# Context values and output projections of a decoder layer as three one-pass products

## The reference

```python
out = jnp.einsum('bhqk,bkhd->bqhd', attn, V).reshape(B, S, D)
return out @ Wo.T + bo                       # the output projection
...
attn = jax.nn.softmax(scores, axis=-1)       # scores of the layernormed x against the context
readout = jnp.einsum('bsm,bmd->bsd', attn, memory_tokens)   # the context values
...
x = x + attention(layernorm(x)); x = x + context(layernorm(x)); x = x + experts(layernorm(x))
```

## Time and profile before

| | us |
|---|---|
| median of 3 runs | 220.63 (220.3 to 221.02) |
| the profiled execution | 220.86, span 219.1 |
| PE busy | 211.4 (96%) |
| DVE busy | 160.7 (73%) |
| ACT busy | 129.6 (59%) |
| POOL busy | 87.5 (40%) |

### The profile page before, as it was taken

The page is one execution under the profiler, slowest core; times in us unless marked ns, Lnnn a source line. Parts: engine busy times, 40 slices in busy tenths (PEclk is TensorE's granted clock), DMA queues, the critical chain, the costliest instruction groups (busy, mean ns, idle before and its releaser), DMA issues.

```text
span 219.1 us, 4397 instructions
## 1 busy us (share of the span) xinstructions
PE 211.4 (96%) x1390; PEld 176.4 (80%) x1390; DVE 160.7 (73%) x440; ACT 129.6 (59%) x249; POOL 87.5 (40%) x77
## 2 busy tenths in 40 slices
PE   7999999999999899999999999999999999999995
PEld 2687766776787689799898898898898898898893
DVE  3469898869558657888998785785785786786754
ACT  2138789859641814468767765665676666666340
POOL 7249989304001110076347625615516516416000
DMA  6795530000000000004331342142141241310002
GB/s 208 297 377 170 145 100 0 0 3 1 3 0 0 0 3 1 0 2 148 144 84 66 140 144 81 63 144 63 80 144 41 102 144 24 120 48 0 0 0 97
DMA packets 8062, 17.45 MB, mean 80 GB/s; under 512 B 960, under 2 KB 3184, under 8 KB 7920
## 3 DMA queue, kind: packets, MB, share of 16 engines
q1 hardware_dynamic: 7616, 16.97, 23.0%
q10 hardware_dynamic: 432, 0.31, 0.5%
HBM read 16.75 MB, written 0.52 MB: 79 GB/s over the span
## 4 chain that ended last, share of the span: by engine, by line
PE 83%; DVE 8%; ACT 4%; issue 3%; POOL 1%; DVEq 0%; ACTq 0%; POOLq 0%
PE PS L1185 35%; PE PS L1201 20%; PE PS L957 3%; PE PS L1069 3%; PE PS L1054 3%; PE PS L945 3%; PE PS L1009 3%; ACT pr L458 2%; PE PS L1042 2%; PE PS L971 2%; PE PS L995 2%; PE PS L1230 2%; PE PS L1022 2%; PE PS L999 1%; DVE masked L741 1%
## 5 line engine op out<-in xcount | busy, mean ns | idle before, releaser
L320 POOL TENSOR_TENSOR WLg<-raw_g,WHg 128x1024 fp32r<-128x1024 f32 x16 | 38.4, 2399 | 69.3 <-ACT WHg L428 65.7
L1185 PE MATMUL PS<-XH,WHg 128*128 128x512 f32 x120 | 47.1, 392 | 0.0
L1185 PE MATMUL PS<-XL,WHg 128*128 128x512 f32 x120 | 46.9, 391 | 0.0
L1185 PE MATMUL PS<-XH,WLg 128*128 128x512 f32 x120 | 46.7, 389 | 0.0
L867 DVE TENSOR_SCALAR pt<-pt 128x512 f32<-128x512 f32 x30 | 23.8, 792 | 20.7 <-ACT pt L552 20.7
L1201 PE MATMUL PS<-WLd,HH 128*128 128x256 f32 x120 | 34.0, 283 | 0.0
L1201 PE MATMUL PS<-WHd,HL 128*128 128x256 f32 x120 | 33.9, 283 | 0.0
L1201 PE MATMUL PS<-WHd,HH 128*128 128x256 f32 x120 | 33.9, 282 | 0.0
L558 ACT ACTIVATE HH<-pt 128x512 fp32r<-128x512 f32 x30 | 18.9, 630 | 18.8 <-DVE pt L871 18.2
L552 ACT ACTIVATE pt<-PS,bup 128x512 f32<-128x512 f32 x30 | 20.6, 687 | 13.3 <-PE PS L1185 13.2
L871 DVE SCALAR_TENSOR_TENSOR pt<-pt 128x512 f32<-128x512 f32 x30 | 24.9, 830 | 4.2 <-DVE pt L867 1.4
(11 more groups left out here) (172 smaller groups left out, 358.5 us busy)
## 6 DMA issues: line engine op xcount, KB each, us to landing
raw_g<-we_d SPq DMA_DIRECT2D x16, 512.0 KB, 4.1
raw_w<-we_d SPq DMA_DIRECT2D x16, 256.0 KB, 2.7
ctxT<-ctxT_d SPq DMA_DIRECT2D x1, 1024.0 KB, 9.4
ctx_sb<-ctx_d SPq DMA_DIRECT2D x1, 1024.0 KB, 11.7
wqkv<-wqkv_d SPq DMA_DIRECT2D x3, 256.0 KB, 3.9
out_d<-x SPq DMA_DIRECT2D x4, 128.0 KB, 1.7
rows<-rows_d SPq DMA_DIRECT2D x1, 264.0 KB, 6.1
x<-x_d ACTq DMA_DIRECT2D x2, 128.0 KB, 2.8
```

Source lines behind the costliest of these rows:

```text
L320: g.tensor_tensor(WLg[slot][:, :, :, :].rearrange("p k g f -> p (k g f)"), raw_g[slot][:, :], WHg[slot][:, :, :, :].rearrange("p k g f -> ...
L1185: i = t.matmul(PS[:, 2 * m + part, :], w[slot][:, k, part, m * P:(m + 1) * P], xx[:, k, :], start=(n == 0), stop=(n == 3 * KD - 1))
```

## The change

- The output projection of both batches and the context values of all four chunks become three one-pass products each: high x high, low x high, high x low (for the context values: high x high and high x low of a chunk first, and its low x high later in a function of its own).
- ScalarE's copies out of PSUM are the same in number and size but now write the high part (att_high, xpt_high).
- VectorE gets seven new subtractions from PSUM for the low parts: one of 128x512 for the attention of batch 0 (`low_att`), two of 128x256 for that of batch 1, and one of 128x512 for each of the four context chunks (`context_low`).
- GpSimd rounds and subtracts wo (128x512) after the router, and the context in two halves of 128x1024 after the second key split and after rstds(1).
- TensorE no longer spreads the context values of chunks 0 and 1 in halves around project(1) and the transposes: it does the high passes of a chunk before and its low pass behind.
- The memory of the raw context and of xT is used again for the low context and for wo's parts. The transfers are not touched.

```diff
+        xpt_high, xpt_low = (sb(n, [P, 2, KM, P], F32R) for n in ("xpt_high", "xpt_low"))
...
@@ GpSimd
             split_router()
+            pool.wait_ge(wo_in, 16)
+            pool.wait_ge(v_ps, NC)
+            g.tensor_copy(wo_high[:, :, :], wo[:, :, :]).then_inc(wo_high_done, 1)
+            pool.wait_ge(wo_high_done, 1)
+            g.tensor_tensor(wo_low[:, :, :], wo[:, :, :], wo_high[:, :, :].bitcast(F32), ALU.subtract).then_inc(wo_low_done, 1)
             split_keys(0)
             masks()
             split_keys(1)
+            def split_context(b):
+
+                pool.wait_ge(ctx_in, 16)
+                chunks = slice(b * KM, (b + 1) * KM)
+                g.tensor_copy(ctx_high[:, chunks, :], ctx_sb[:, chunks, :]).then_inc(ctx_high_done, 1)
+                pool.wait_ge(ctx_high_done, b + 1)
+                g.tensor_tensor(ctx_low[:, chunks, :], ctx_sb[:, chunks, :], ctx_high[:, chunks, :].bitcast(F32), ALU.subtract
+                                ).then_inc(ctx_low_done, 1)
+
+            split_context(0)
             rstds(1)
+            split_context(1)
...
@@ VectorE
+            def low_att(b, n, bank, tokens):
+
+                if b == 1:
+                    dve.wait_ge(proj_done, QC)
+                dve.wait_ge(attT_done[b], n)
+                count = tokens.stop - tokens.start
+                v_.tensor_tensor(att_low[:, :, tokens.start - b * S:tokens.stop - b * S], PS[:, bank, 0:KD * count].rearrange("p (k n) -> p k n", k=KD),
+                                 att_high[:, :, tokens].bitcast(F32), ALU.subtract).then_inc(att_low_done[b], 1)
+
...
+            def context_low(c):
+
+                dve.wait_ge(xpt_done, c + 1)
+                if c >= 2:
+                    dve.wait_ge(xav_done, c - 1)
+                v_.tensor_tensor(xpt_low[:, c % 2].rearrange("p h q -> p (h q)"), PS[:, XT_BANK[c], :],
+                                 xpt_high[:, c % 2].rearrange("p h q -> p (h q)").bitcast(F32), ALU.subtract).then_inc(xlow_done, 1)
...
                 if v == TAIL - 1:
                     outputs(0, 0, 7)
+                if v == TAIL:
+                    low_att(0, 1, 7, slice(0, S))
...
+            context_low(0)
             context_weight(0)
             context_weight(1)
+            context_low(1)
+            low_att(1, 1, 7, slice(S, S + P))
+            low_att(1, 2, 0, slice(S + P, T))
             residual(1, 0, PS[:, 6, 0:D])
...
             normalise(x3, 3, (0, 1))
+            context_low(2)
             context_weight(2)
             context_weight(3)
+            context_low(3)
...
@@ TensorE
-                    pe.wait_ge(attT_done[b], 1 if b == 0 else j + 1)
+                    pe.wait_ge(att_low_done[b], 1 if b == 0 else j + 1)
+                    n = 0
                     for k in range(KD):
-                        i = t.matmul(places[j], attT[:, k, c * P:(c + 1) * P], wo[:, k, :],
-                                     start=(k == 0), stop=(k == KD - 1))
+                        for xx, w in ((att_high, wo_high), (att_low, wo_high), (att_high, wo_low)):
+                            chunk = j if xx is att_low else c
+                            i = t.matmul(places[j], xx[:, k, chunk * P:(chunk + 1) * P], w[:, k, :], start=(n == 0), stop=(n == 3 * KD - 1))
+                            n += 1
...
-            def context_values(c, blocks=range(KM)):
+            def context_values(c):
                 pe.wait_ge(xpt_done, c + 1)
-                for j in blocks:
...
+                pe.wait_ge(ctx_low_done, c // QC + 1)
+                for j in range(KM):
+                    for w in (ctx_high, ctx_low):
+                        t.matmul(PS[:, XV_BANK[c], 0:D], xpt_high[:, c % 2, j, :], w[:, (c // QC) * KM + j, :],
+                                 start=(j == 0 and w is ctx_high), stop=False)
+
+            def context_values_low(c):
+                pe.wait_ge(xlow_done, c + 1)
+                for j in range(KM):
+                    i = t.matmul(PS[:, XV_BANK[c], 0:D], xpt_low[:, c % 2, j, :], ctx_high[:, (c // QC) * KM + j, :],
+                                 start=False, stop=(j == KM - 1))
+                i.then_inc(xav_done, 1)
...
-            pe.wait_ge(ctx_in, 16)
-            context_values(0, range(0, KM // 2))
+            context_values(0)
             project(1, [PS[:, 6, 0:D], PS[:, 5, 0:D]])
-            context_values(0, range(KM // 2, KM))
-            context_values(1, range(0, KM // 2))
+            context_values_low(0)
+            context_values(1)
             for j in range(QC):
                 pe.wait_ge(xn_done, NC + QC + j + 1)
                 turn_chunk(xn, QC + j, (7, 3)[j])
-            context_values(1, range(KM // 2, KM))
+            context_values_low(1)
...
             context_values(2)
+            context_values_low(2)
             context_values(3)
+            context_values_low(3)
```

More of the change, by code:

```diff
@@ L65, in decoder_layer @@
         rest_of_wqkv = sb("rest_of_wqkv", [P, KD, D])
-        ctx_sb = sb("ctx_sb", [P, B * KM, D])
+        raw_ctx = ExitStack()
+        ctx_sb = raw_ctx.enter_context(nc.sbuf_tensor("ctx_sb", [P, B * KM, D], F32))
+        raw_ctx.close()
+        ctx_low = sb("ctx_low", [P, B * KM, D], F32R)
+        ctx_high = sb("ctx_high", [P, B * KM, D], F32R)
+        xpt_high, xpt_low = (sb(n, [P, 2, KM, P], F32R) for n in ("xpt_high", "xpt_low"))
         wo = sb("wo", [P, KD, D])
@@ L95, in decoder_layer @@
         xn = sb("xn", [P, NC, D])
-        xT = sb("xT", [P, KD, T])
+        turned_x = ExitStack()
+        xT = turned_x.enter_context(nc.sbuf_tensor("xT", [P, KD, T], F32))
+        turned_x.close()
+        wo_high, wo_low = (sb(n, [P, KD, D], F32R) for n in ("wo_high", "wo_low"))
         kT = sb("kT", [P, KD, T])
@@ L107, in decoder_layer @@
         att = sb("att", [P, NC, D])
-        attT = sb("attT", [P, KD, T])
+        att_high = sb("att_high", [P, KD, T], F32R)
+        att_low = sb("att_low", [P, KD, S], F32R)
         x2 = sb("x2", [P, NC, D])
@@ L163, in decoder_layer @@
         xp = [keys_flat[:, i * M:(i + 1) * M] for i in range(2)]
-        xpt = [keys_flat[:, (2 + i) * M:(3 + i) * M].rearrange("p (c q) -> p c q", q=P) for i in range(2)]
         cth, ctl = [keys_high0[:, :, :], keys_high1[:, :, :]], [keys_low[:, b * KD:(b + 1) * KD, :] for b in range(B)]
@@ L183, in decoder_layer @@
         attT_done = [sem(f"attT_done{b}") for b in range(B)]
+        att_low_done = [sem(f"att_low_done{b}") for b in range(B)]
+        wo_high_done, wo_low_done = sem("wo_high_done"), sem("wo_low_done")
         q_ps, k_ps, v_ps = sem("q_ps"), sem("k_ps"), sem("v_ps")
@@ L205, in decoder_layer @@
         out_done = sem("out_done")
+        xlow_done, ctx_high_done, ctx_low_done = sem("xlow_done"), sem("ctx_high_done"), sem("ctx_low_done")
         dbias_zero, dbias_split, score3_zero, score_parts = (sem(n) for n in ("dbias_zero", "dbias_split", "score3_zero", "score_parts"))
@@ L471, in context_take @@
                     act.wait_ge(xav_done, c - 1)
-                a.activation(xpt[c % 2].rearrange("p h q -> p (h q)"), PS[:, XT_BANK[c], :], ACT.Copy
+                a.activation(xpt_high[:, c % 2].rearrange("p h q -> p (h q)"), PS[:, XT_BANK[c], :], ACT.Copy
                              ).then_inc(xpt_done, 1)
@@ L515, in _ @@
                     act.wait_ge(lnT_done, 3)
-                    a.activation(attT[:, :, 0:S], turned(7, slice(0, S)), ACT.Copy).then_inc(attT_done[0], 1)
+                    a.activation(att_high[:, :, 0:S], turned(7, slice(0, S)), ACT.Copy).then_inc(attT_done[0], 1)
                 if v == NV:
@@ L525, in take_chunk @@
                              ).then_inc(done, 1)
-            take_chunk(attT, 2, 7, 5, attT_done[1])
-            take_chunk(attT, 3, 0, 6, attT_done[1])
+            take_chunk(att_high, 2, 7, 5, attT_done[1])
+            take_chunk(att_high, 3, 0, 6, attT_done[1])
             context_take(1)
@@ L1098, in _ @@
                 if v == TAIL + 1:
-                    pe.wait_ge(wo_in, 16)
+                    pe.wait_ge(wo_low_done, 1)
                     project(0, [PS[:, 7, j * D:(j + 1) * D] for j in range(QC)])
```

## The result

The changed kernel takes 222.11 us in the median of 6 runs (221.84 to 222.24) against 220.49 of the kernel before in the same comparison: ratio 1.007, 95% interval 1.006 to 1.008, so 1.6 us slower. The profiled execution has a span of 220.5 against 219.1.

A forecast was written before the change was run, and what follows sets the result against it. TensorE was taken to bound the kernel (83% of the chain), with VectorE nearly as late in the touched stages. Terms 0.33 + 1.20 - 0.30 = +1.23 on 220.86 gave 222.1, stated as 222.0; 8-in-10 range 221.1 to 222.8 us.

The forecast's parts named there:

- Cost of a product: TensorE's replaced products: three one-pass instructions take 0.359 us, 0.20 first and 0.1195 each later, against 0.419 for one float32 product.
- the whole possible gain: TensorE over both projections and four context chunks: 1.4 us less work, called all the change could gain.
- Batch 0, +0.33: Batch 0's projection: waits for VectorE's new subtraction, starts at 45.39 instead of 44.77, ends 0.33 us later.
- Batch 1, +1.20: Batch 1's projection: low attention queues behind chunk 1's low part on VectorE; residual 1.20 us later, arriving whole at context scores.
- Chunks 2 and 3, -0.30: Context values of chunks 2 and 3: TensorE ends 0.40 us earlier, but VectorE is late, so only 0.30 is gained.
- GpSimd at no cost: GpSimd's splits of wo and context: at most 3.3 and 4.7 us, fitting into 12 us of waiting, so free.
- The sum: Whole kernel: 0.33 + 1.20 - 0.30 = +1.23 us, from 220.86 profiled to 222.1, given as 222.0.
- The hidden low parts: Rival at batch 1's projection: low attention delivered before 63.44, TensorE's saving shows, 219.5 us; chance 0.08.
- The absorbed shift: Rival between batch 1's projection and chunk 2's context scores: only half of 1.20 arrives, 221.5 or 221.2 us; chance 0.17.
- rival 3: GpSimd's new work holds VectorE's small instructions: 0.1 us for the rstd scaling, up to 0.6 more, 222.7; chance 0.13.
- The rule of a quarter: Replaced TensorE products: three passes for float32's four would save a quarter, 2.5 us, where the rows gave one seventh, 1.4.
- What should show: Profile signs: TensorE idle 0.6 before project(0), 1.2 before project(1); residual at 65.9; wrong if chunk 2's scores under 1 us later.

The follow-up runs named there:

- e7: Changed kernel with VectorE's weights of chunks 2 and 3 moved ahead of context_low(2): 221.78 us, ratio 1.0048 to the kernel before.
- e1: Changed kernel with context_low(1) moved behind batch 1's two low attention parts on VectorE: 220.92 us against 220.67 before, ratio 1.0013.
- e2: Changed kernel with VectorE's list of batch 1 put in order of readiness: 220.66 us against 220.65 before, ratio 0.9996.
- e4: Changed kernel with only the output projections in three products, context values float32 in halves as before: 220.97 us, ratio 1.0015 to the kernel before.
- e5: Changed kernel with GpSimd's second context split moved ahead of rstds(1): 221.94 us, ratio 1.0061 to the kernel before.
- e8: Changed kernel with transposes before project(0), batch 1's list by readiness, chunk 2 and 3 weights first, early second split: 219.61 us against 220.65 before, ratio 0.9950.

## Why the prediction was right, point by point

- **Cost of a product.** Forecast 0.20 and then 0.1195 for each instruction. The projection's twelve run from 45.50 to 47.01, 1.51 as forecast, chunks 2 and 3 need 2.97 (75.56 to 78.53) for 2.95. TensorE's busy time fell by 1.4, which agrees but is too coarse to prove it. What the step had wrong is that 1.4 were "the whole possible gain": behind a last one-pass product the result is ready 0.2 us sooner as well (e7). The prediction had this in its own 77.0 for TensorE's results in chunks 2 and 3 (in e7 the output came 8.71 after E, which is 77.02 if E is put at the 68.31 of before). That is 0.59 before 77.59, but it called only 0.40 the gain there.
- **Batch 0, +0.33.** Measured +0.44 (15.77 against 15.33). The step held; the size was off by TensorE's start: 45.50 comes 0.15 after VectorE's end at 45.35, where the earlier trace rows had shown 0.05 for such a hand-over. The wait of 0.73, less the 0.29 that the projection saves, is the 0.44.
- **Batch 1, +1.20.** Measured +1.32 in C-D, D-E unchanged, so it arrived whole. The missing 0.12 are VectorE's start 0.11 after ScalarE's end (64.05 after 63.94, taken as 0.02) and 1.01 instead of 0.98 from the projection's start to the residual. That the idle time reads 1.20, as forecast, is a coincidence: the forecast counted from where the next product could start, the row from the end of the last one. Counted as in the forecast it is 1.36 (65.13 less 63.65 + 0.12) against 1.18, since TensorE came 0.08 earlier and the low part 0.09 later than forecast, beside the shift of 0.42 from batch 0. e1, e2 and e4 show the cause from three sides.
- **Chunks 2 and 3, -0.30.** Measured -0.34; e7 shows that VectorE is the bound there.
- **GpSimd at no cost.** It was done with the first half of the context at 45.04 and rstds(1) came 7.74 us of idle time later; the second half ended at 57.00. The forecast's bounds were wide, 3.3 for wo and 4.7 for a half, where 1.9 and 3.5 were measured. e5: no change.
- **The sum.** +1.23 forecast, +1.39 in the table, +1.4 in the spans, +1.6 in the medians. The last 0.2 lie within what the start of the executions varies by, and the later comparisons point to the kernel before: its median is 220.49 in 6 runs there, and 220.65 to 220.67 in 20 to 27 runs, against which 222.11 is 1.4 to 1.5 more. That the forecast time, 222.0, lies 0.1 from the measured one is luck in part: 1.23 on the 220.49 of the comparison would be 221.7.
- **The rivals.** The hidden low parts (219.5) needed them ready before 63.44; e2 is that case, and gave 220.66, not 219.5, because batch 0's wait stays, batch 1's saving is used up by the four more instructions ahead of the projection, and VectorE holds back part of the gain in chunks 2 and 3. With all waits filled (e8) it is 219.6. The absorbed shift did not occur: D-E is 3.90 and 3.91.
- **GpSimd's hold, rival 3.** The prediction put it at 0.1 or so for the small scaling instruction. It was 1.2 (1.37 instead of 0.16): the right instruction, with a size wrong by a factor of ten. That it cost nothing is luck, since it fell into a gap of 1.35 us with 0.1 to spare. Both rows show the same pattern: the clamp ended at 103.47 beside a subtraction that ended at 103.19, the scaling at 57.03 beside one that ended at 57.00. This agrees with the lock in the Trainium skill, page "SBUF — State Buffer", section "Who interferes with whom", which lasts for the whole instruction of the engine that has it; by that the hold could be as long as the subtraction, and not the 0.1 that the prediction read from it. No run shows whether the scaling ran in a two-port mode.
- **The rule of a quarter.** The Trainium skill, page "FP8 and Floating Point Precision", section "TensorE Precision Notes", gives true FP32 four passes; the saving of a quarter that the prediction worked out from it did not come. Three one-pass products took 0.36 where the float32 one took 0.42, one seventh less: a single one cost 0.1195 and not a quarter of 0.419, which would be 0.105.
- **What should show.** Idle 0.73 instead of 0.6 before project(0), residual at 66.14 instead of 65.9, the rest as written; the context scores of chunk 2 came 1.73 later (70.04 after 68.31), where less than 1 would have made the prediction wrong.

## What to carry to other kernels

Cheaper products on the engine that bounds the kernel bring nothing where they make it wait for one more link of a relay: write down, for every new operand, which engine delivers it and what stands ahead of it in that engine's list. A list in the order of readiness, and ready work put ahead of the instruction that must wait, turned the same change from 1.6 us slower into 1.0 us faster, of which 0.2 to 0.3 come from the order alone, without the change. Measure the parts alone as well: here they were -0.3 and +0.4, and their meeting in one list was the 1.2 that mattered.

## What was not expected of the hardware

A scaling of 128x2 elements on VectorE, 0.16 us by itself, took 1.37 us beside a GpSimd subtraction of 128x1024 (54.61 to 57.00) and ended with it. And a hand-over from VectorE to TensorE was 0.05 us in one place (before, 54.84 to 54.89) and 0.15 in another (after, 45.35 to 45.50), while the same products in batch 1 started about 0.06 after theirs (65.13, after 64.66 + 0.41); what makes the difference was not tested.
